# A recurrent mixer and expert layer on one core: convolution in two blocks, experts in token layout, the router for batch 0 first, and all jobs in a new order

## What is computed

```python
xn = layernorm(x)
# branch 1: gated long convolution over the 512 tokens of each batch
u, v = split(silu(xn @ uv_w))                       # 128 + 128 features
# filter for lags -511..511: a small network (32 wide, 3 layers + output) of the lag, times 0.99**|lag|
s = (u * causal_and_anticausal_convolution(v, filter)) @ o_w
# branch 2: mixture of experts, one pair of experts (of 8) for a whole batch
rw = softmax(xn.mean(axis=1) @ Wr + br)             # one row per batch
top-2 of rw, softmax over the two -> cw
h  = gelu(xn @ W1[e] + b1[e])                       # 128 -> 512, for both experts
out = sum_j cw[j] * (h_j @ W2[e_j] + b2[e_j])       # 512 -> 128
g = silu(layernorm(out + xn) * gamma + beta)
result = x + s * g
```

## Time and profile before

| what | value |
|---|---|
| median of 3 runs | 260.24 us (257.44 to 264.85) |
| span of the profiled execution, first to last instruction | 255.3 us |
| own time of the profiled execution | not given apart from the three runs; the runs lie 2.1 to 9.5 us above the span, the median 4.9 us |
| instructions in the profile | 3013 |
| busy: PE, DVE, POOL, ACT | 216.9, 136.8, 106.1, 99.8 us |

### The profile page before, as it was taken

One profiled execution on the slowest core, in us unless ns is written; L12 is line 12 of the kernel. 1 busy time (PEld: TensorE's weight loads), 2 busy tenths in 40 slices (PEclk: granted clock), 3 DMA queues, 4 the chain that ended last, 5 costly groups with the idle time before them and its releaser, 6 DMA issues.

```text
span 255.3 us, 3013 instructions
## 1 busy us (share of the span) xinstructions
PE 216.9 (85%) x928; PEld 157.9 (62%) x928; DVE 136.8 (54%) x373; ACT 99.8 (39%) x172; POOL 106.1 (42%) x105
## 2 busy tenths in 40 slices
PE   0457987758949999999895999999999999999950
PEld 0336977755625787767564778777757667756640
DVE  2999956414170300666787288548674452533374
ACT  2225556737637524332232222332262444353400
POOL 0555534061492400358996024229865205301310
PEclk9999999955988999999999999999999999999995
DMA  7317600335263230020203310420415404010011
GB/s 208 90 58 261 277 0 3 98 112 150 89 175 154 82 85 0 5 77 0 50 32 87 80 41 3 123 82 1 125 32 155 105 0 126 0 41 0 0 41 41
DMA packets 25015, 19.71 MB, mean 77 GB/s; under 512 B 1368, under 2 KB 22528, under 8 KB 24616
## 3 DMA queue, kind: packets, MB, share of 16 engines
q1 hardware_dynamic: 24624, 19.23, 25.2%
q10 hardware_dynamic: 376, 0.30, 0.5%
HBM read 17.43 MB, written 2.10 MB: 76 GB/s over the span
## 4 chain that ended last, share of the span: by engine, by line
PE 62%; DVE 16%; POOL 7%; issue 7%; ACT 4%; DMA 3%; SPq 1%; POOLq 0%; DVEq 0%; ACTq 0%
PE bank L1080 19%; PE bank L1111 10%; PE bank L924 8%; PE bank L925 8%; PE bank L926 8%; PE bank L1003 3%; PE bank L1135 2%; DVE xn L684 2%; DVE prod L727 2%; DVE stats L665 2%; POOL layer_r L578 2%; DMA x_ring<-in_L_attn_x 1%; POOL w_lo L610 1%; PE bank L1123 1%; DMA w_raw<-in_L_ffn_W 1%
## 5 line engine op out<-in xcount | busy, mean ns | idle before, releaser
L499 ACT ACTIVATE h_ring<-bank,b_sel 128x512 f32<-128x512 f32 x64 | 43.9, 688 | 67.8 <-PE bank L926 67.7
L1080 PE MATMUL bank<-h_ring,w_s 128*128 128x512 f32 x128 | 66.6, 604 | 0.0
L924 PE MATMUL bank<-xT_hi,w_hi 128*128 128x512 f32 x64 | 41.4, 647 | 0.7 <-ACT h_ring L499 0.7
L610 POOL TENSOR_TENSOR w_lo<-w_raw,w_hi 128x512 fp32r<-128x512 f32 x16 | 21.0, 1334 | 37.2 <-ACT w_hi L453 37.2
L1111 PE MATMUL bank<-inv_sb,Y 128*128 128x256 f32 x128 | 29.3, 380 | 3.7 <-DVE conv L870 2.5
L1111 PEld LDWEIGHTS bank<-inv_sb,Y 128*128 128x128 f32 x128 | 24.0, 190 | 10.6 <-issue 5.7
L1080 PEld LDWEIGHTS bank<-h_ring,w_s 128*128 128x128 f32 x128 | 24.7, 193 | 6.6 <-issue 1.0
L926 PE MATMUL bank<-xT_hi,w_lo 128*128 128x512 f32 x64 | 26.1, 408 | 0.0
L925 PE MATMUL bank<-xT_lo,w_hi 128*128 128x512 f32 x64 | 26.1, 408 | 0.0
L602 POOL TENSOR_TENSOR Y<-prod 128x512 f32<-128x512 f32 x8 | 10.9, 1365 | 35.3 <-DVE prod L862 35.3
L858 DVE TENSOR_TENSOR prod<-bank,A_sb 128x512 f32<-128x512 f32 x8 | 5.5, 692 | 29.2 <-PE bank L926 29.2
(11 more groups left out here) (153 smaller groups left out, 429.0 us busy)
## 6 DMA issues: line engine op xcount, KB each, us to landing
x_ring<-in_L_attn_x SPq DMA_DIRECT2D x16, 256.0 KB, 3.6
w_raw<-in_L_ffn_W SPq DMA_DIRECT2D x16, 256.0 KB, 2.8
w_s<-in_L_ffn_W SPq DMA_DIRECT2D x16, 256.0 KB, 2.9
Y<-table_lag SPq DMA_DIRECT2D x1, 2048.0 KB, 9.2
out_dram<-x_ring SPq DMA_DIRECT2D x8, 256.0 KB, 2.3
inv_sb<-table_fwd SPq DMA_DIRECT2D x1, 1024.0 KB, 4.8
inv_sb<-table_inv SPq DMA_DIRECT2D x1, 1024.0 KB, 4.7
c<-table_c ACTq DMA_DIRECT2D x1, 202.0 KB, 2.8
```

What stands on the lines that cost most here:

```text
L499: nc.scalar.activation(h_ring[:, n % NH], H_PS[n % 2][:], ACT.Gelu, bias=b1_sel[:, c, j, b:b + 1]).then_inc(h_done, 1)
L610: nc.gpsimd.tensor_tensor(w1_lo[:, b % 2, j], w1_raw[:, j], w1_hi[:, b % 2, j], ALU.subtract).then_inc(w1_split, 1)
L924: nc.tensor.matmul(out_ps, w_hi, m_hi, start=start, stop=False)
L1080: nc.tensor.matmul(OUT_PS[:], w2_s[:, b % 2, j, c], h_ring[:, n % NH], start=False, stop=(i == HT - 1)).then_inc(w2_mm, 1)
```

## The change

The file is rewritten. What each part does now:

- **Convolution in two blocks of 256 tokens.** A transform of length 512 over each block (`forth_before`, `forth_after`, eight jobs of each, two batches and half of the frequencies at a time), with three filter spectra in place of one (same block, and the two cross terms), combined in the manner of a three-product multiplication. No high and low halves: these matmuls are plain F32. The products on DVE are 6 per unit (`product_before`, `product_after`, `product_both`, eight units) and a sum in PSUM; POOL adds in `third`, `second` and `spectra` (5 additions of 512 elements per unit). ACT copies one of the two spectra out of PSUM (`v1_copy`). `back` is 8 F32 matmuls of 128 columns per batch (2 parts by 2 blocks by 2 halves of the frequencies).
- **The filter.** One more representation: the 32 features of each lag are transformed (`lag_features`, `feature_spectra`: 2 transposes, 2 F32 matmuls of 512 columns), then multiplied by the sign-weighted output weights (`filter_re`, `filter_im`: for each of two, F32 matmuls of 384 and of 256 columns). The lag table shrinks from 2 MB to 512 KB, the two transform tables from 1 MB to 256 KB each.
- **Experts in token layout.** `expert_out` uses four 128-token slices of h as weights and the W2 slice as the moving operand: four F32 matmuls of 128 columns per chunk. `transpose_y` and the two identity matmuls go. DVE adds xn plus the mixed b2 (`experts_out`, `bias_mix`; POOL's `residual`), ACT normalizes (`gate_norm`, 28 instructions of 128 elements) and scales W2 (`w2_scale`), which DVE did.
- **The router on all 128 partitions,** in groups of batches (0), (1), (2, 3), (4 to 7). Batch 0 does not wait for its transposed block: its mean comes from x and the row roots (`first_mean`). b2 rows and the mixing weights are fetched and computed per group. The softmax uses Tanh in place of Exp.
- **The lag network** uses Tanh with two DVE operations in place of Silu on ACT.
- **x is kept** for all eight batches; the reloads go.
- **W1's low half** alternates between DVE and POOL.
- **All jobs of all five engines** stand in five tables of positions; jobs of both parts are mixed, and the first expert chunks stand ahead of the projections of most batches.

The core of the diff:

```diff
-SPECTRUM_AT = [9, 9, 10, 11]
-FORTH_AT = [14, 16, 18, 20, 30, 32, 34, 36]
-BACK_AT = [22, 24, 26, 28, 42, 45, 50, 63]
+GROUPS = [(0, 1), (1, 2), (2, 4), (4, 8)]
+MIXES = [(0, 1), (1, 4), (4, 8)]
+LO_ON = ["dve"] * 1 + ["pool"] * 1 + ["dve"] * 1 + ["pool"] * 1 + ["dve"] * 1 + ["pool"] * 1 + ["dve"] * 1 + ["pool"] * 1 + ["dve"] * 1 + ["pool"] * 1 + ["dve"] * 1 + ["pool"] * 1 + ["dve"] * 1 + ["pool"] * 1 + ["dve"] * 1 + ["pool"] * 1
+SP_AT = {
+    "x": [0, 1, 3, 4, 5, 6, 8, 9],
+    "lag": [2],
+    "wr": [7],
...
+DVE_AT = {
+    "rw": [0],
+    "xs": [1, 2, 6, 11, 26, 39, 40, 44],
+    "xnm": [3, 5, 18, 19, 29, 43, 50, 51],
+    "rm": [4],
...
+    "rank": [15, 16, 36, 67],
...
+PE_AT = {
+    "tx": [1, 6, 15, 19, 34, 42, 55, 70],
...
+    "pu": [8, 13, 17, 40, 71, 74, 77, 80],
+    "pv": [9, 14, 18, 36, 41, 73, 79, 82],
+    "logits": [10, 11, 30, 81],
...
+    "h": [21, 22, 23, 24, 25, 27, 39, 43, 44, 47, 48, 51, 52, 54, 57, 62, 65, 67, 68, 76, 91, 92, 94, 96, 97,
...
+    "f0": [83, 100, 114, 134, 147, 160, 176, 192],
+    "f1": [85, 98, 116, 127, 145, 161, 171, 184],
+    "back": [126, 130, 155, 165, 183, 188, 206, 207],
+    "s": [133, 136, 162, 178, 189, 197, 208, 209],
...
+            def first_mean(n):
+                pe.wait_ge(rstd_done, 1)
+                pe.wait_ge(wrc_done, 1)
+                for t in range(NT):
+                    last = nc.tensor.matmul(R0_PS[:, 8:9], x_all[:, 0, t], rstd[:, 0, t:t + 1],
+                                            start=(t == 0), stop=(t == NT - 1))
+                last.then_inc(mean0_ps, 1)
...
             def expert_out(n):
...
                 pe.wait_ge(h_done, n + 1)
-                j, c = i // FC, i % FC
-                nc.tensor.matmul(OUT_PS[:], w2_s[:, b % 2, j, c], h_ring[:, n % NH],
-                                 start=False, stop=(i == HT - 1)).then_inc(w2_mm, 1)
+                for t in range(NT):
+                    tok = slice(t * P, (t + 1) * P)
+                    last = nc.tensor.matmul(OUT_PS[b % 2][:, tok], h_ring[:, n % NH, tok], w2_s[:, i % NW2, c],
+                                            start=(n % HT == 0 and t == 0), stop=(n % HT == HT - 1),
+                                            skip_group_check=True)
+                last.then_inc(out_ps, 1)
...
+            def forth(m, n, ps):
+                q, kc = m // 2, m % 2
+                for ri in range(2):
+                    last = nc.tensor.matmul(ps[:, ri * BLK:(ri + 1) * BLK], fwd_sb[:, ri, kc],
+                                            fold[:, q, ri, n].rearrange("p b d -> p (b d)"),
+                                            start=True, stop=True)
+                return last
...
+            def product_both(m):
+                dve.wait_ge(v1_done, m + 1)
+                dve.wait_ge(p3_done, m + 1)
+                nc.vector.tensor_tensor(V0_PS[:], V0_PS[:], v1_s[:], ALU.add).then_inc(sum_done, 1)
+                dve.wait_ge(sum_done, m + 1)
+                product(m, 0, V0_PS[:]).then_inc(p1_done, 1)
...
+            def spectra(m):
+                q, kc = m // 2, m % 2
+                pool.wait_ge(p1_done, m + 1)
+                step(nc.gpsimd.tensor_tensor(prod[:, 0], prod[:, 0], prod[:, 1], ALU.add))
+                if q >= 2:
+                    pool.wait_ge(eo_ps, 2 * (q - 1))
+                pool.wait_ge(t3_done, m + 1)
+                pool.wait_ge(t2_done, m + 1)
+                for n, with_third in ((0, 2), (1, 4)):
+                    last = nc.gpsimd.tensor_tensor(Y[:, q % 2, kc, n].rearrange("p r b d -> p (r b d)"),
+                                                   prod[:, 0], prod[:, with_third], ALU.add)
+                last.then_inc(Y_done, 1)
```

More of the change, by code:

```diff
@@ new lines, in store @@
+            def store(b):
+                sp.wait_ge(res_dve if RES_ON[b] == "dve" else res_pool, nth(RES_ON, RES_ON[b], b))
+                sp.dma_start(out_v[b], x_all[:, b]).then_inc(out_done, 16)
+            jobs = {"x": load_x, "uvw": load_uvw, "wr": load_router, "b1": load_b1, "lag": load_lag,
+                    "tables": load_transforms, "gate": load_gate, "w1": fetch_w1, "w2": fetch_w2,
+                    "b2": fetch_b2, "store": store}
+            for what, n in in_order(SP_AT):
+                jobs[what](n)
@@ L551, in _ @@
+            for what, n in in_order(ACT_AT):
+                jobs[what](n)
         @block.gpsimd
@@ L652, in _ @@
+            for what, n in in_order(POOL_AT):
+                jobs[what](n)
         @block.vector
@@ L915, in _ @@
[L915 to L918 removed]
+                    last = nc.vector.scalar_tensor_tensor(out=z_s[:, b % 2, t], in0=y_s[:, b % 2, t],
+                                                          scalar=ymv[:, b, t, 0:1], in1=gam[:],
+                                                          op0=ALU.subtract, op1=ALU.mult)
@@ new lines, in weigh @@
+            def weigh(b):
+                dve.wait_ge(s_ps, b + 1)
+                dve.wait_ge(g_done, b + 1)
+                g = flat(th[:, b % 2])
+                nc.vector.tensor_tensor(g, S_PS[:], g, ALU.mult).then_inc(s_read, 1)
+            def result(b):
+                dve.wait_ge(s_read, b + 1)
+                nc.vector.tensor_tensor(x_all[:, b], x_all[:, b], th[:, b % 2], ALU.add).then_inc(res_dve, 1)
+            jobs = {"xs": x_stats, "xnm": normalize, "xlo": x_lower, "uvw": uvw_lower, "lo": w1_lower,
+                    "rw": position_weights, "rm": position_matrices, "eps": layer_eps, "spread": layer_spread,
+                    "lnorm": layer_norm, "lsilu": layer_silu, "wrc": router_weights, "mean0": first_mean,
+                    "rank": rank, "b1t": bias_columns, "pick": bias_pick, "shift": mix_shift,
+                    "share": mix_share, "mix": mix_weights, "ow": out_weight, "p3": product_before,
+                    "p2": product_after, "p1": product_both, "eo": even_odd, "uc": convolved,
+                    "b2": bias_mix, "xb": residual, "o": experts_out, "ys": gate_sum, "aff": gate_affine, "g": gate,
+                    "sg": weigh, "res": result}
@@ L919, in _ @@
+            for what, n in in_order(DVE_AT):
                 jobs[what](n)
@@ new lines, in logits @@
+            def logits(g):
+                first, end = GROUPS[g]
+                if g == 0:
+                    pe.wait_ge(mean0_done, 1)
+                    nc.tensor.matmul(R0_PS[:, 16:16 + E], bcast(mean0[:], [P, P]), wrc[:], start=True,
+                                     stop=True).then_inc(logit_ps, 1)
+                else:
+                    pe.wait_ge(xlo_done, end)
+                    for b in range(first, end):
+                        last = nc.tensor.matmul(RT_PS[:, (b - first) * E:(b - first + 1) * E],
+                                                bcast(xsum[:, b:b + 1], [P, P]), wrc[:], start=True, stop=True)
+                    last.then_inc(logit_ps, 1)
```

1570 lines of the change are left out of this document (815 added, 755 removed), and 20 rows, old and new, of tables (DVE_AT, PE_AT, POOL_AT, SP_AT).

## The result

| | before | after |
|---|---|---|
| median of 4 runs each, taken together | 262.42 us (257.44 to 264.85) | 215.7 us (215.39 to 215.88) |
| ratio after / before | | 0.832 (95% interval 0.826 to 0.839) |
| span of the profiled execution | 255.3 us | 213.3 us |

In some executions a kernel takes longer at a lower granted clock; the ratio and the medians of the experiments leave these out, so 0.832 stands for 215.7 over about 259 and not over 262.42.

A forecast was written before the change was run, and what follows sets the result against it. PE's own work at full clock was taken as the bound, beside start and end: 32 + (170 - 12) = 190, span 200 with the tail, plus clock 4 and stalls 8 = 212, plus 4.9: 217 us; range 200 to 238.

The forecast's parts named there:

- Prices on PE: PE's jobs priced at full clock from trace distances: 170 us in sum, 12 of it before the first `hidden`.
- Weight loads of 128 columns: Rival: 384 more loads in `expert_out` not hidden, +65, time 282 us; chance 0.06, shared with other mechanisms costing 45 us.
- Where dense work begins: Start: index at about 26 us, W1 usable 5.1 later, first `hidden` at 32 where it was near 57.
- Stalls: Dense part: PE, DVE and POOL in fixed order lose 0 to 1.8 us per round; 1.0 taken, 8 us.
- round of 13.8: PE's us per round, eight rounds: 8 `hidden`, 8 `expert_out` on most, one unit of `forth`, a `back`, a `mixed`.
- The clock: One stretch of lowered clock as the dense part begins after sparse work: 4 us.
- The tail: End, behind the last `expert_out`: add, statistics, root, `aff`, DVE's remaining operations, store and handovers, 15.3 us.
- From span to time: The old span stood 4.9 us under the median of 260.24; this took span 212 to time 217.
- the vector bound: Rival: DVE and POOL bound, 15.6 a round for 13.8, and 10 us before the first unit; time 233; chance 0.22.
- The no-stall case: Rival: no stall and the clock stays up; span 200, time 205 or 202 us; chance 0.10.
- The late index: Rival: DVE's queue or the loads delay the router's index to 36 us, +10, time 227; no separate chance given.

The follow-up runs named there:

- the 512-column form: Changed kernel with `expert_out` put back to one F32 matmul of 512 columns, W2 as weights, in place of four of 128: 216.2 us against 215.7 and 216.4.
- the twelve loads: Changed kernel with 12 small loads on SP's queue between the router's index and the first W1 fetch: 216.6 us against 215.7 and 216.4.

## Why the prediction was right

The time was 215.7 for 217, the span 213.3 for 212. But the nearness of the number is in good part luck: a start 10 us too early was paid for by stalls, a clock term, a tail and an offset that were all too large. By the steps:

- **Prices on PE: right.** Busy 186.8 (180 to 190 was the sign), `expert_out`'s x8 groups 0.89. After the first `hidden` PE did 160.2 us of work at full clock where the sum had 158: 199.8 - 42.3, less 1.0 of waits and 1.6 for the half pace up to 45.8, plus the 5.3 that stand behind the last `expert_out`. The whole was a little more under-priced, since a third projection, about 2 us, lay before it. (The F32R matmul of 128 columns is 0.111, not 0.106: the distance behind the first of the eleven is 0.06.)
- **Weight loads of 128 columns: the rival fell.** They cost 2.2 us, by the 512-column form. The trace's price per column held for these F32 matmuls, and not the rule of the Trainium skill, "TensorE: Matmul & The Clock Gate", section "Back-to-back issue gap", by which they would have cost some 80.
- **Where dense work begins: failed.** The forecast said 32, the trace 42.3, its own mark for "wrong". Three terms: the index at 29.6 instead of 26 (DVE began at 9.25 for the 7.5 assumed, and L752 took 3.97 beside POOL's 3.22 us, which I had priced at 1.1 "less overlap"); index to usable W1 6.0 instead of 5.1; and 5.8 us that I had not seen at all: in PE's table a layer product (1.2 us), a third projection (3.9 at half pace), and a transpose with a layer variance (1.6) stand between 35.6 us and the first `hidden`, 6.7 in all where the sum had 0.9. The table was in the diff; I followed the chain of the index and not PE's own list. That the index had slack is shown by the twelve loads (6.4 us later, under 1 lost); that DVE's first job and POOL's long operation were on the path is shown by moving each (-1.6 to -2.4, and -1.8).
- **Stalls: over-sized.** I took 1.0 a round, 8 in all; PE waited for about 1 us between 42 and 200. The parts were as predicted: POOL 96% busy, DVE's operations on two SBUF inputs at 0.93 to 1.14. The round of 13.8 was right too (107.6 us for eight units, 13.4 each, from the first `forth` to the last `expert_out`), though its bracket was not: what it lists adds to 17.1, while only 44 `hidden` and 50 `expert_out` were left for the eight rounds. The inference was wrong: as it seems, the order leaves each unit enough distance that POOL can be full and PE not wait. No run tests that with another order. Some 2 us more on POOL fit, 8.7 do not.
- **The clock: a cost there was, but in another place.** I had 4 us for a fall as the dense part begins. It is instead the start that runs at half pace, to 45.8. After 42 us that is 1.6; before it, it is a part of the late `hidden`.
- **The tail:** 13.5 for 15.3; the eight `aff` instructions took 2.3 for 2.7, and the rest of DVE's queue and the store were shorter.
- **From span to time: over-sized.** I added 4.9, the median of the kernel before less the span of its shortest execution, which mixes its scatter into an offset. Each execution with both numbers on record lies 1.7 to 2.5 above its own span; here the median is 2.4 above 213.3.

In sum for the end of the last `expert_out`: forecast 196.7 (184.7 + 12), measured 199.8. Start +10.3, stalls -7, clock -2.4, PE's work +2.2: +3.1. With the tail's -1.8 that is the span's +1.3, and with the offset's -2.5 the time's -1.2.

Of the rivals, the vector bound (233) did not come, but one addition more per unit shows it near: the time follows POOL from some 2 us on. The no-stall case (205) was right about the stalls and missed by its start. The late index (227) named a delay of 10 us with the wrong owner; it cost what it said, and the stalls that weren't there paid for it.

## What to carry to other kernels

Price a new order by each engine's own list, and not only by the chain of data that you think gates it: here what stood ahead in PE's table, not the index, set the first dense work. Work taken from the bounding engine becomes time only while the next engine leaves room and while no wait lets the clock fall: the same kind of cut gave 15 of 28 us in the old order, and 2.2 us off PE in the new one gave nothing. And before a busy-share sum gets a stall term, look for distance in the order: an engine at 96% that is served early enough stalls nobody. To see how near it is, add a little work to it, and read from the trace how much was really added.

## What the hardware showed that was not expected

- The granted-clock row reads 1.00 from 24 to 36 us in the kernel after (below), while F32R matmuls of 512 columns start 0.42 apart, twice the 0.228 of full rate. With work put at the head of PE's list, matmuls at the same distance have a row of 0.50. So at the start the row alone can't be read as the rate; the distance between starts can. By that distance PE was at its lower level, 1.2 GHz, up to about 45 us in the kernel after, although it was busy for 11.1 of 12 us from 24 to 36; in the kernel before it left it near 31 us. What sets this difference stays open.

```profile
24.00:36.00 12.00, 11.10 (x45) 10.10 (x46) 6.77 (x29) 5.58 (x14) 4.53 (x7) 1.00 0.22 75
```

- A `tensor_scalar` group on SBUF data of four instructions took 3.97 us in place of 1.11 beside one POOL operation of 3.22 that began just behind its start, and 1.11 again when that operation was moved away, while operations of DVE with an input in PSUM kept 0.68 us beside a POOL that was 96% busy. The Trainium skill, "SBUF — State Buffer", section "Who interferes with whom", says that a DVE operation in a two-port mode, `tensor_scalar` among them, and POOL shut each other out for the whole instruction, and that one with at most one SBUF input outside such a mode does not contend. The trace agrees, with these numbers.
- One such long POOL operation in DVE's critical stretch cost 1.8 us of the kernel's time; 19 us of short ones on POOL in the dense part cost at most 1.5.
